# Filter stage of a fused graph layer: half the feature transposes, a first layer in two parts, and small attention products dealt out one by one

## The reference

```python
# graph part: a filter for each edge from its 20 features f_ij
h = shifted_softplus(f_ij @ Wf1 + bf1)          # [40000,20] @ [20,128]
W = (h @ Wf2 + bf2) * rcut_ij[:, None]          # [40000,128] @ [128,768], 512 columns are needed
m_s = s2 * W[:, :2 * F]
...
agg = jax.ops.segment_sum(x_ij, idx_i, num_segments=n)
# attention part, 8 heads of 64
q = jax.nn.softmax(q, axis=-1)
k = jax.nn.softmax(k, axis=-1)
context = jnp.einsum('bhnd,bhne->bhde', k, v)
out = jnp.einsum('bhnd,bhde->bhne', q, context)
```

## Time and profile before

| | |
|---|---|
| median of the three runs | 1289.22 us |
| span of the profiled execution, first to last instruction | 1359.2 us |
| filter stage in it | 77 to 548 us |
| message stage in it | 600 to 1155 us |
| busy in the span: PE, DVE, ACT, POOL | 1232.9, 1074.1, 829.4, 878.9 us |

### The profile page before, as it was taken

How to read it: one execution, slowest core, us unless ns; L and a number is a source line. 1 busy time by engine, 2 the same in 40 slices (tenths; PEclk the granted TensorE clock), 3 DMA queues, 4 the chain that set the end, 5 groups by cost and what they waited for, 6 DMA issues and landing times.

```text
span 1359.2 us, 16348 instructions
## 1 busy us (share of the span) xinstructions
PE 1232.9 (91%) x4175; PEld 724.8 (53%) x4175; DVE 1074.1 (79%) x1972; ACT 829.4 (61%) x1821; POOL 878.9 (65%) x793
## 2 busy tenths in 40 slices
PE   5998889998988998799999999999999999975995
PEld 3566566666665666343444444444444444764882
DVE  6858777788777897568999999899999997567425
ACT  3676666666666766056777777777777775754330
POOL 8356666666666677548888788888888882043650
PEclk8989999999889998899999999999999999976996
DMA  9246765865877875678988988888999981544457
GB/s 266 69 160 243 267 228 221 290 226 206 284 247 262 286 274 211 234 275 295 316 314 305 315 302 307 295 312 308 312 312 306 311 282 46 203 148 139 162 175 224
DMA packets 106612, 337.65 MB, mean 248 GB/s; under 512 B 16870, under 2 KB 17806, under 8 KB 100376
## 3 DMA queue, kind: packets, MB, share of 16 engines
q0 software_dynamic: 57456, 188.80, 38.9%
q1 hardware_dynamic: 49064, 147.81, 33.2%
HBM read 211.25 MB, written 125.30 MB: 248 GB/s over the span
## 4 chain that ended last, share of the span: by engine, by line
PE 74%; DVE 10%; another core or an unknown queue 5%; issue 4%; DMA 3%; ACT 3%; POOL 1%; SPq 0%; DVEq 0%; POOLq 0%; ACTq 0%
PE PS L2272 20%; PE PS L2277 20%; PE PS L2208 12%; PE PS L2399 5%; DVE RR L1561 3%; PE PS L2081 2%; PE PS L2143 2%; PE PS L2091 2%; PE PS L2161 2%; PE PS L2059 2%; PE PS L2169 1%; PE PS L2206 1%; POOL expert_inputs L1000 1%; DVE h_low L1554 1%
## 5 line engine op out<-in xcount | busy, mean ns | idle before, releaser
L970 POOL DMA_INDIRECT RR<-node_table,RR x322 | 446.1, 1385 | 121.5 <-issue 76.6
L1228 ACT ACTIVATE RR<-RR 128x256 f32<-128x256 f32 x966 | 394.4, 495 | 200.6 <-PE PS L2277 159.1
L933 POOL DMA_INDIRECT edge_records<-RR x316 | 318.0, 1006 | 171.9 <-issue 88.9
L2272 PE MATMUL PS<-RR 128*125 128x512 f32 x644 | 291.6, 596 | 4.9 <-DVE RR L1738 2.7
L2277 PE MATMUL PS<-RR 128*125 128x512 f32 x644 | 289.6, 592 | 0.0
L1561 DVE TENSOR_TENSOR RR<-PS,RR 128x512 f32<-128x512 f32 x237 | 161.2, 685 | 91.4 <-PE PS L2208 54.9
L2272 PEld LDWEIGHTS PS<-RR 128*125 128x125 f32 x644 | 120.7, 189 | 163.1 <-issue 147.4
L2277 PEld LDWEIGHTS PS<-RR 128*125 128x125 f32 x644 | 120.9, 188 | 155.7 <-issue 155.7
L2208 PE MATMUL PS<-wf_high,h_high 128*128 128x512 f32 x316 | 152.2, 482 | 14.0 <-issue 7.7
L1738 DVE TENSOR_TENSOR RR<-RR 128x1536 f32<-128x1536 f32 (+1 forms) x81 | 140.9, 1740 | 0.0
L2208 PE MATMUL PS<-wf_low,h_high 128*128 128x512 f32 x316 | 129.0, 408 | 0.0
(11 more groups left out here) (345 smaller groups left out, 1871.8 us busy)
## 6 DMA issues: line engine op xcount, KB each, us to landing
RR<-edge_records SPq DMA_DIRECT2D x48, 1040.0 KB
expert_inputs<-RR SPq DMA_DIRECT2D x8, 2313.0 KB
RR<-edge_records SPq DMA_DIRECT2D x27, 520.0 KB
RR<-edge_records SPq DMA_DIRECT2D x15, 780.0 KB
RR<-in_L_ffn_beta_w SPq DMA_DIRECT2D x8, 1024.0 KB
expert_w_raw<-in_L_ffn_expert_w SPq DMA_DIRECT2D x8, 1024.0 KB, 8.8
RR<-edge_records SPq DMA_DIRECT2D x31, 260.0 KB
edge_records<-RR POOLq DMA_INDIRECT x322
```

Of the source, the lines that this page charges most:

```text
L933: g.indirect_dma_start(out=rec_dram, out_offset=place, in_=ST[:, j, :], in_offset=None).then_inc(scattered[c], 16)
L970: g.indirect_dma_start(out=GB[q % GBS][:, t, 1:5, :].rearrange("p k n -> p (k n)"), out_offset=None, in_=tab_dram, in_offset=bass.Indirect ...
L1228: last = a.activation(message_slot(q)[:, t, k:k + 5:4, :], GB[q % GBS][:, t, 0:k + 3:k + 2, :], ACT.Copy, scale=record_slot(q)[:, t, 4 * C ...
L2272: te.matmul(PS[0:NT, 2 * (r % PSS), :], OH[q % OHS][:, t, 0:NT], GB[q % GBS][:, t, 1:5, :].rearrange("p k n -> p (k n)"), start=(n == 0), ...
```

## The change

Two columns of edges share one transpose: a column's features now take 64 words (`FW`): a 1 at 0, high parts at 1 to 20 and again at 21 to 40, low parts at 41 to 60, and a 1 at 61. Two columns make the 128 words of a transpose, so a step has two transposes and ACT copies 128x256. The first layer becomes two products of 256 columns (`odd` 0 and 1), each with weights that are zero in the half of the other column; `wf1_parts` has two such blocks, made with a few small operations of POOL, ACT and DVE. The second layer reads a column's place in the hidden values through `hidden_edges`. The first layer's weights are loaded ten times by SP's queue in place of six times by POOL's, and six small loads on SP come after the first two tiles of the node table. The query transposes and the context products stand singly, one behind each column of r = 4 and r = 5.

```diff
-        def feature_halves(m):
-            return Fst[:, m % 2, :, :].rearrange("p c (g w) -> p c g w", g=2)
-        def twice(columns):
-            return columns.unsqueeze(2).to_broadcast([P, STEP, 2, R])
+        FW = P // 2
+        FT = STEP * FW
+        BIAS_LOW, HIGH_LOW, HIGH_HIGH, LOW_HIGH, BIAS_HIGH = 0, 1, 1 + R, 1 + 2 * R, 1 + 3 * R
+        fT = rounded("fT", fT_at, [P, 2, FT], r2_base)
+        Fst = rounded("feature_columns", fst_at, [P, 2, STEP // 2, P], r2_base)
+        def hidden_edges(j):
+            place = (j % 2) * 2 + j // 2
+            return slice(place * P, (place + 1) * P)
...
@@ sync
+            for first in (0, FW):
+                for part in (HIGH_LOW, HIGH_HIGH, LOW_HIGH):
+                    sp.dma_start(wf1[first + part:first + part + R, :], Wf1).then_inc(wf_in, 16)
+                for row in (BIAS_LOW, BIAS_HIGH):
+                    sp.dma_start(wf1[first + row:first + row + 1, :], bf1.rearrange("(o n) -> o n", o=1))\
+                        .then_inc(wf_in, 16)
...
@@ gpsimd
-            for part in range(4):
-                g.dma_start(wf1[32 * part:32 * part + R, :], Wf1).then_inc(wf_in, 16)
...
+            g.tensor_scalar(wf1_low, wf1[:, :], wf1_is_low, None, ALU.mult)
@@ scalar
-                a.activation(fT[:, c % 2, :], PS[:, 0, :], ACT.Copy).then_inc(fT_ready, 1)
+                a.activation(fT[:, c % 2, :], PS[:, 0, 0:FT], ACT.Copy).then_inc(fT_ready, 1)
@@ vector
-                v.tensor_tensor(feature_halves(m)[:, :, :, 32:32 + R], twice(Fe[:, m // CHUNK % 2, first:first + STEP, :]),
-                                feature_halves(m)[:, :, :, 0:R].bitcast(F32), ALU.subtract).then_inc(f_staged, 1)
+                v.tensor_tensor(feature_columns(m)[:, :, LOW_HIGH:BIAS_HIGH], Fe[:, m // CHUNK % 2, first:first + STEP, :],
+                                feature_columns(m)[:, :, HIGH_HIGH:LOW_HIGH].bitcast(F32), ALU.subtract)\
+                    .then_inc(f_staged, 1)
@@ tensor
-                for j in range(STEP):
-                    last = te.matmul(PS[:, 0, j * P:(j + 1) * P], Fst[:, c % 2, j, :], ident_r[:, :], start=True, stop=True)
+                for pair in range(STEP // 2):
+                    last = te.matmul(PS[:, 0, pair * P:(pair + 1) * P], Fst[:, c % 2, pair, :], ident_r[:, :],
+                                     start=True, stop=True)
...
-                te.matmul(PS[:, 1 + c % 2, :], wf1_parts[:, :], fT[:, c % 2, :], start=True, stop=True)\
-                    .then_inc(z_psum, 1)
+                for odd in range(2):
+                    last = te.matmul(PS[:, 1 + c % 2, odd * FT:(odd + 1) * FT], wf1_parts[:, odd, :], fT[:, c % 2, :],
+                                     start=True, stop=True)
+                last.then_inc(z_psum, 1)
...
-                elif 0 <= t < NB and r == 4 and j == 2:
-                    query_transposes(t)
-                elif 0 <= t < NB and r == PER - 1 and j == 2:
-                    context(t)
+                elif 0 <= t < NB and r == 4:
+                    query_transpose(t, j)
+                elif 0 <= t < NB and r == PER - 1:
+                    context(t, j)
```

More of the change, by code:

```diff
@@ L327, in gps_layer @@
         c2(2048)
-        wf1_parts = rounded("wf1_parts", c2.at, [P, P])
-        c2(P)
-        assert c1_early <= c2.at - P <= acc_at
+        wf1_parts = rounded("wf1_parts", c2.at, [P, 2, P])
+        c2(2 * P)
+        assert c1_early <= c2.at - 2 * P and c2.at <= acc_at
         in_hidden = 4 * 512 // RC1
@@ L867, in _ @@
                 .then_inc(rcut_in, 16)
[L868 removed]
+            g.dma_start(wf2raw, Wf2[:, 0:4 * C]).then_inc(b2_in, 16)
             g.dma_start(b2raw, bf2.rearrange("(o n) -> o n", o=1)[:, 0:4 * C].to_broadcast([2, 4 * C]))\
                 .then_inc(b2_in, 16)
[L871 to L875 removed]
             pool.wait_ge(edge_in, 16 * 6)
@@ L882, in _ @@
             step(g.memset(Fst[:, :, :, :].bitcast(F32), 0.0))
-            for half_of in range(2):
-                g.memset(Fst[:, :, :, P // 2 * half_of + R:P // 2 * half_of + R + 1].bitcast(F32), 1.0)
+            every = Fst[:, :, :, :].rearrange("p s c n -> p (s c n)").rearrange("p (c w) -> p c w", w=FW)
+            for row in (BIAS_LOW, BIAS_HIGH):
+                g.memset(every[:, :, row:row + 1].bitcast(F32), 1.0)
+            g.memset(wf1_parts[:, :, :].bitcast(F32), 0.0)
+            for k, end in enumerate((HIGH_HIGH, FW, FW + HIGH_HIGH)):
+                below = g.affine_select(out=wf1_marks[:, k:k + 1], in_=ones[:, 0:1], compare_op=ALU.is_gt, fill=0.0,
+                                        base=end, pattern=[[0, 1]], channel_multiplier=-1)
+            step(below)
+            step(g.tensor_tensor(wf1_is_low, wf1_marks[:, 0:1], wf1_marks[:, 1:2], ALU.subtract))
+            step(g.tensor_tensor(wf1_is_low, wf1_is_low, wf1_marks[:, 2:3], ALU.add))
+            g.tensor_scalar(wf1_sign, wf1_is_low, -2.0, 1.0, ALU.mult, ALU.add)
             g.memset(b2hl[:, :].bitcast(F32), 0.0)
@@ L1084, in stage_f @@
                 first = m % CHUNK * STEP
-                a.activation(feature_halves(m)[:, :, :, 0:R], twice(Fe[:, m // CHUNK % 2, first:first + STEP, :]), ACT.Copy)\
-                    .then_inc(f_high, 1)
+                high_twice = feature_columns(m)[:, :, HIGH_LOW:LOW_HIGH].rearrange("p c (g r) -> p c g r", g=2)
+                columns = Fe[:, m // CHUNK % 2, first:first + STEP, :]
+                a.activation(high_twice, columns.unsqueeze(2).to_broadcast([P, STEP, 2, R]), ACT.Copy).then_inc(f_high, 1)
             def exp_q(t):
@@ L1515, in _ @@
             stage_f_low(0, 1)
-            lower = slice(P // 2, P)
-            v.tensor_tensor(wf1_parts[lower, :], wf1[lower, :], wf1_parts[lower, :].bitcast(F32), ALU.subtract)\
-                .then_inc(wf2_l, 1)
+            for half_of in range(2):
+                rows = slice(FW * half_of, FW * (half_of + 1))
+                last = v.scalar_tensor_tensor(wf1_parts[rows, half_of, :], wf1_parts[rows, half_of, :].bitcast(F32),
+                                              wf1_sign[rows, :], wf1_low[rows, :], ALU.mult, ALU.add)
+            last.then_inc(wf2_l, 1)
             v.tensor_tensor(wf2_low[:, :, :], wf2[:, :, :], wf2_high[:, :, :].bitcast(F32), ALU.subtract)\
@@ L2093, in key, with query_transpose, context @@
                     last.then_inc(k_psum, 1)
[L2095 to L2106, removed]
+            def query_transpose(t, k):
+                if k == 0:
+                    pe.wait_ge(q_norm, t + 1)
+                last = te.transpose(PS[:, 6, k * NT:(k + 1) * NT], QW[0:NT, k * P:(k + 1) * P], idn)
+                if k == KD - 1:
+                    last.then_inc(qT_psum, 1)
+            def context(t, k):
+                if k == 0:
+                    pe.wait_ge(k_norm, t + 1)
+                last = te.matmul(PS[:, 7, k * P:(k + 1) * P], VN[0:NT, t, k * P:(k + 1) * P],
+                                 KN[0:NT, t % 2, k * P:(k + 1) * P], start=True, stop=True)
+                if k == KD - 1:
+                    last.then_inc(ctx_psum, 1)
             def context_wo(k):
```

34 lines of the change are left out of this document (20 added, 14 removed).

## The result

| | runs | median us (lowest to highest) | ratio to before, 95% |
|---|---|---|---|
| before | 4 | 1289.10 (1287.92 to 1290.62) | |
| changed | 4 | 1279.44 (1277.76 to 1280.24) | 0.9919 [0.9899, 0.9939] |
| changed, a second series (`e8_after_again`) | 6 | 1276.00 (1274.02 to 1280.19), before 1287.43 | 0.9910 [0.9891, 0.9928] |

The change saves 9.7 us, or 0.8%; by the interval it is 7.9 to 13.0 us. The second series has 11.4 us. The forecast was 1284.0 us, a saving of 5.2. Two executions that were slow at a low granted clock, one of before in the second series (1786.3 us, clock 0.649) and one of `e9_fewer_before` (1953.5 us, 0.555), are in no ratio.

A forecast was written before the change was run, and what follows sets the result against it. PE's order of work was taken to set most of the end, with POOL's scatters close behind in the filter stage. Transposes -10.6 and ACT's copy -1 gave -11.6 us; some half, 5.2, from 1289.2 gave 1284.0 us, range 1266 to 1294.

The forecast's parts named there:

- The likeliest case: Filter stage: PE's saving comes through in part, 3 to 12 us, runs at 1277 to 1286 us; chance 0.42.
- The transposes, 10.6 us on the path: Filter stage, PE: feature transposes hold 21.2 us of the chain; halving their number saves half, 10.6 us.
- 15.8 us: Filter stage, PE: two fewer transposes save 0.20 us per step, over 79 steps 15.8 us of PE time.
- The first layer, 0.23 us for the two: First layer on PE: two 256-column products take 0.23 us together, like one of 512; ends -1.6 and +12.2 us in all.
- ACT's copy 1 us, DVE's low parts 0: Filter stage: ACT's smaller copy saves 1 us; DVE's halved low parts count 0, at most 12.6 us of DVE time.
- The dealing 0, the wait for the keys 0, the late query copies 0: r = 4 and r = 5: each counted 0; other ends rival C, 5 us for the keys, 7 us for query copies.
- rival C: Between r = 4 and 5: bursts of small matmuls cause the stalls, 26 us in six tiles; 1258 us; chance 0.14.
- The prologue 0: Prologue: first-layer weights on SP's queue arrive at 35 us, POOL ends at some 42, before ACT's 48; 0 us.
- The 70 us between the profile and the runs: Filter stage: unnamed stalls of 47 us would cover most of the 70; the runs' stage estimated at 410 to 440 us.
- for the runs I take some half of it: Last step: of 11.6 us saved in the profiled execution, 5.2 us taken, since POOL's 401 to 413 us are near.
- Rival B: Filter stage: POOL paces it already and PE waits longer for the ring; -2 to +2 us, 1289; chance 0.22.
- The two sums per tile: Filter stage, a tile's six steps: PE has 29.7 us of work and POOL 30.5 to 31.4; the two called level.

The follow-up runs named there:

- e9_fewer_before: The kernel before without the second layer's third product of each column (low part of h by high part of weights), left out of the result: 1277.95 us, 0.9927.
- e1_deal_only: The kernel before with only the query transposes and context products dealt out, one behind each column of r = 4 and r = 5: 1288.83 us, 1.0006.
- e3_four_transposes: The changed kernel with each step's two feature transposes issued twice, so PE has four again; all else of the change stays: 1286.91 us, 0.9992.
- e10_levels_later: The changed kernel with DVE's five small run-table steps moved from r = 5 to r = 2 of the next tile: 1279.08 us, 0.9933.
- e4_split_layer1: The kernel before with only its first layer split into two products of 256 columns, same weights and result: 1289.07 us, 1.0004.
- e2_bursts_again: The changed kernel with query transposes and context products in one burst each behind column 2 again: 1277.48 us, 0.9925.
- e5_fewer_products: The changed kernel without the second layer's third product of each column (low part of h by high part of weights), left out of the result: 1275.06 us, 0.9896.
- e0_before: The kernel before, unchanged, profiled a second time because the first profile's span was 1359.2 us: span 1285.7 us, its own run 1287.5 us.
- e6_pool_more: The changed kernel with one small memset on POOL, waited for, ahead of each step's four scatters: 1334.68 us, 1.0355.

## Why the prediction came out as it did

The likeliest case was right: faster by PE's transposes, 3 to 12 us. The steps one by one:

- **The transposes, 10.6 us on the path.** Right in place and nearly in size, though the 21.2 us behind it were read from the disturbed execution; the same share in the second profile, 4.0% of 471 us, would have given 9.4. Laid side by side, the bias products of the changed kernel run ahead of those of before by 0.20 to 0.23 us in each step in which PE has no gap (5.42 to 5.19 us at r = 1, 5.02 to 4.80 at r = 2, 5.81 to 5.60 at r = 3, medians over the tiles). By tile 8, r = 3, they are 11.4 us ahead. Of these, 1.5 us come in the first three steps and 1.5 at m = 39 (8.4 to 6.9 us); the latter step takes 6.8 us in `e1_deal_only` too, which is no faster, so it isn't the transposes'. `e3_four_transposes`, which gives the two transposes back and loses the gain, shows that it is they.
- **Where the rest of 15.8 us went.** Two places. In tiles 0 to 3, r = 4 is 0.30 us shorter (4.15 to 3.85), but r = 5 is 0.42 us longer (6.10 to 6.52): behind the last key product the path is DVE's, and it takes as long as before. The chain from one bias product at r = 4 to the one at the next tile's r = 0 (tile 1, changed kernel, 143 to 154.2 us):

```profile
by line: DVE RR L1586 27.6%; issue 13.8%; DVE h_low L1579 11.4%; DVE small L1485 6.3%; DVE RR L1495 6.2%; DVE RR L1569 5.7%; DVE small L1493 5.3%; PE PS L2236 4.2%; PE PS L2116 4.0%; DVE small L1451 3.7%; DVE small L1494 1.9%; DVE small L14
```

  In these tiles a tile takes 31.2 us in the changed kernel, which is just what POOL takes for its 24 scatters (24 x 1.30), so a shorter path there gains little, as `e10_levels_later` shows. And from tile 8, r = 4 on, the ring of four steps paces it: 11.4 us ahead become 7.9 ten steps later (m = 64) and 9.45 at the last step. The chain there goes through POOL's scatters and the landing of the last of them to DVE's copy of line 1559:

```profile
356.02 0.96 POOL edge_records L953
356.98 0.30 issue
357.28 0.96 POOL edge_records L953
...
358.55 9.14 DMA edge_records<-RR
...
367.71 0.18 DVE RR L1559
```

- **The first layer, 0.23 us for the two.** Right: 0.24 us, and `e4_split_layer1` shows no price.
- **ACT's copy 1 us, DVE's low parts 0.** Right as far as can be told: 365 ns for the copy, and `e3_four_transposes`, which keeps both, is at 0.9992 and has all that the change holds beside the transposes: 1.0 us, with an interval of -0.6 to +2.7. The low parts fell by 81 of 318 ns for half the elements; the "at most" held.
- **The dealing 0, the wait for the keys 0, the late query copies 0.** Right as far as can be told (`e1_deal_only`, `e2_bursts_again`). The stalls at the bursts, which gave rival C its 26 us, belonged to the disturbed execution.
- **The prologue 0.** Right: the first bias product stands at 76.05 us, before 76.07.
- **The 70 us between the profile and the runs.** Right that they were for the most part stalls which the runs don't have (56 of 73.5 us in L; the rest lies outside it), and that the stage of the runs takes 410 to 440 us: 409.9 us between bias products.
- **The step that was mis-sized is the last one, "for the runs I take some half of it".** It took PE's saving as good only down to POOL's 401 to 413 us and the stage as near to it, so 5.2 us of 11.6. The floor is 410.3 us (`e5_fewer_products`), inside that range, but the stretch to be compared with it is L, 424.2 us before. That is 14 us more, of which 11 are POOL's waits and 3 the scatters' own time, which differs that much from profile to profile. So there were 11 us of room, and the change took 9.8 us of POOL's waits away. The two numbers were not of one kind: the stage's 410 to 440 us run from bias product to bias product, and the scatters run on for 18.8 us behind the last of those (486.0 to 504.8). Against its own stretch, the floor took little. The sum without the halving, 11.6 us, would have been nearer to the 9.7 and 11.4 us measured.

Rival B, POOL as the pace already, had the mechanism but not the moment: POOL waited 11 us inside its stretch before, and waits 1 us in the changed kernel, which by this stands at its floor. The two sums per tile, 29.7 us for PE and 30.5 to 31.4 for POOL, had the order wrong. In `e0_before` a tile takes 32.0 us (tiles 1 to 3), mostly since r = 5 takes 6.1 us and not 3.6 + 0.9: DVE's work stands in that step, and the sum had PE's alone. That it was above POOL's 31.2 us fits that taking time from PE paid.

## What to carry to other kernels

An engine that works at a fixed rate behind a ring is a floor, and its room is read from its own idle time between its first and last instruction, not from the engine ahead of it: here 107.1 us before, of which 96.1 are pauses that stay. Before work is taken from the engine that leads the chain, take away far too much of it in one run, even if part of the result is then left out: it shows how much there is to be had, and here the change had already got most of it. And where the profiled execution is some per cent longer than the runs, profile the kernel once more before its stalls are read as the kernel's.

## What the runs showed of the hardware

- A memset of 0.18 us on POOL between two scatters costs 0.72 us, since the scatter behind it, which waits for its end, starts 0.84 us later instead of 0.30 (`e6_pool_more`, 76 of the 79). Behind a conversion in the prologue it is 0.34 us.
- The pause between two scatters is 0.30 us, whether their semaphores have long been there (line 953) or the program has them wait for nothing (the six of line 939, at 66.75 us and after).
- The scatters' DMAs land 2.7 to 9.7 us after their issue (median 4.1) in the changed kernel, for those whose landing the profile gives. The long ones decide when the ring frees a place: in the piece shown above it is 9.14 us.
- Two products of 256 columns and one of 512 take the same time, 0.24 and 0.23 us, at a granted clock of 0.98 to 0.99 of 2.4 GHz in the stage.
- A float32 product stands in the trace as two matmul records, the eight of the four context products among them: a key product of 512 columns takes 0.86 us in its two, where one of the rounded type takes 0.23 us in its single one. How the engine divides the work within them isn't shown.
- One profiled execution held 47 us of stalls of unnamed releaser in its filter stage's chain, which none of the twelve other profiles has.
